# A cross-attention and feed-forward kernel: its query projection, the start of its score loop and its quantised weights rearranged

## What is computed

```python
q = (xq @ Wq.T + bq).reshape(B, N, HEADS, HEAD_DIM).transpose(0, 2, 1, 3)   # xq = layernorm(x)
k = (xk @ Wk.T + bk)...            # xk = xv = ctx_1024, 16 heads of 8
scores = jnp.einsum('bhnd,bhmd->bhnm', q, k) * scale
weights = jax.nn.softmax(scores, axis=-1)
...
def lpbq_dequant(w):               # blocks of 32 columns, 4 bits
    s = jnp.maximum(jnp.max(jnp.abs(wb), axis=-1, keepdims=True) / qmax, 1e-12)
    wq = jnp.clip(jnp.round(wb / s), -qmax - 1.0, qmax) * s
```

## Time and profile before

| | |
|---|---|
| device time, median of 3 runs | 823.46 us (821.6 to 823.87) |
| the profiled execution | 828.05 us, span 826.3 us |
| busy share of the span | PE 84%, DVE 71%, ACT 65%, POOL 50% |
| score loop, first and last start of its exponentials (L627) | 54.2 to 387.8 us |
| clock granted to TensorE, mean of the span | 0.923 |

### The profile page before, as it was taken

One profiled execution on the slowest core, in us unless ns is written; L12 is line 12 of the kernel. 1 busy time (PEld: TensorE's weight loads), 2 busy tenths in 40 slices (PEclk: granted clock), 3 DMA queues, 4 the chain that ended last, 5 costly groups with the idle time before them and its releaser, 6 DMA issues.

```text
span 826.3 us, 24071 instructions
## 1 busy us (share of the span) xinstructions
PE 697.6 (84%) x8999; PEld 498.9 (60%) x8999; DVE 589.1 (71%) x1092; ACT 537.1 (65%) x1164; POOL 415.1 (50%) x492
## 2 busy tenths in 40 slices
PE   5777999999999999997805688888788885899997
PEld 2255777777777777775402478777677783344443
DVE  4975788887888888887786667677777655566663
ACT  3354677777777777765452698789988872455554
POOL 1859577777777777700000135444445430466664
PEclk8898999999999999999856979899988896899999
DMA  6315544444444444230400405432540440212100
GB/s 198 106 38 164 143 126 133 131 130 132 129 132 129 131 130 132 66 71 8 183 0 25 207 2 176 173 119 79 205 184 3 155 155 2 75 39 77 38 1 23
DMA packets 26545, 85.75 MB, mean 104 GB/s; under 512 B 5780, under 2 KB 7316, under 8 KB 26468
## 3 DMA queue, kind: packets, MB, share of 16 engines
q1 hardware_dynamic: 26472, 84.77, 32.5%
HBM read 65.46 MB, written 0.46 MB: 80 GB/s over the span
## 4 chain that ended last, share of the span: by engine, by line
PE 51%; DVE 15%; POOL 12%; ACT 9%; issue 7%; SPq 3%; DMA 2%; POOLq 0%; DVEq 0%; ACTq 0%
POOL ctx_lo L601 8%; PE ps L1341 8%; PE ps L1358 7%; PE ps L1372 7%; PE ps L1605 5%; ACT c_prob L766 4%; PE ps L1328 4%; PE ps L1589 3%; PE ps L1317 2%; PE ps L1377 2%; ACT w0T L766 2%; SPq L439 2%; DVE tile_max L853 1%; PE ps L1623 1%; DVE amax_part L1077 1%
## 5 line engine op out<-in xcount | busy, mean ns | idle before, releaser
L853 DVE TENSOR_REDUCE tile_max<-ps 128x1 f32<-128x500 f32 x336 | 214.7, 674 | 52.0 <-PE ps L1341 51.2
L627 ACT ACTIVATE probs<-ps 125x896 f32<-125x896 f32 x192 | 175.3, 916 | 95.5 <-PE ps L1358 94.5
L1341 PE MATMUL ps<-k_hi,qdiag 128*128 128x500 f16 x336 | 130.4, 390 | 7.7 <-DVE tile_max L853 6.5
L766 ACT ACTIVATE c_prob<-ps,c_bias,row_scale 125x56 f32<-125x56 f32 x384 | 116.1, 479 | 3.0 <-DVE c_bias L1164 2.7
L578 POOL TENSOR_TENSOR c_prob<-c_prob,c_weight 125x672 f32<-125x672 f32 x32 | 41.9, 1312 | 133.7 <-DVE c_weight L1178 133.7
L1358 PE MATMUL ps<-qstack,kstack 98*125 98x224 f16 x768 | 107.1, 263 | 0.4
L601 POOL TENSOR_TENSOR ctx_lo<-ctx_hi,ctx_lo 128x448 f16<-128x448 f32 x64 | 71.9, 1124 | 70.5 <-ACT ctx_lo L811 70.5
L1358 PEld LDWEIGHTS ps<-qstack,kstack 98*125 98x125 f16 x768 | 86.6, 137 | 21.3 <-ACT probs L627 2.8
L1372 PE MATMUL ps<-probs,v_aug 125*32 125x168 f32 x1536 | 75.4, 314 | 3.3 <-ACT probs L627 2.5
L1659 PE MATMUL ps<-ctx_lo 128*128 128x448 f16 x192 | 68.5, 357 | 6.6 <-DVE ctx_hi L1276 2.8
L534 POOL TENSOR_TENSOR rows_in<-rows_in 125x768 f32<-125x768 f32 (+2 forms) x96 | 68.8, 717 | 7.5
(11 more groups left out here) (264 smaller groups left out, 1706.3 us busy)
## 6 DMA issues: line engine op xcount, KB each, us to landing
row_tiles<-in_ctx_rows_wide SPq DMA_DIRECT2D x40, 774.0 KB, 5.7
ctx<-in_ctxT SPq DMA_DIRECT2D x16, 750.0 KB, 5.4
rows_in<-in_ctx_rows SPq DMA_DIRECT2D x16, 750.0 KB
kstack<-k_hi SPq DMA_DIRECT2D x128, 93.8 KB, 3.2
kstack<-k_lo SPq DMA_DIRECT2D x64, 93.8 KB, 3.1
ctx_hi<-in_wg SPq DMA_DIRECT2D x8, 256.0 KB, 2.7
ctx_hi<-in_wu SPq DMA_DIRECT2D x8, 256.0 KB, 3.0
ctx_hi<-in_wd SPq DMA_DIRECT2D x8, 256.0 KB, 3.4
```

What stands on the lines that cost most here:

```text
L627: nc.scalar.activation(probs[c % RING_P][0:CH, :].rearrange("p (k w) -> p k w", k=2), score_tile(c)[0:CH], ACT.Exp, scale=float(HD) ** -0. ...
L766: last = nc.scalar.activation(c_prob[n % PROBS][:, c, :], ps[0:CH, 2 * (n % 2) + c // 6, bass.ts(c % 6, TOK)], ACT.Exp, bias=c_bias[n % 2] ...
L853: nc.vector.reduce_max(tile_max[:, u % MAXT, u // MAXT:u // MAXT + 1], ps[:, MAXB + (u + p) % 2, 0:KCOLS], AX.X).then_inc(max_done, 1)
L1341: nc.tensor.matmul(ps[:, MAXB + (u + p) % 2, 0:KCOLS], qdiag[p][:, bass.ts(t, 128)], k_hi[p][:, bass.ts(j, KCOLS)], start=True, stop=True) ...
```

## The change

- The queries are projected once. `q_lo`, the low part, is written by VectorE beside q_hi. The repeated rows of `q_rep` are filled by DMAs: eight issued by ACT (from q_hi) and four by SP (from q_lo). `wq_rep` and `bq_rep` and their loads are gone.
- On ACT `context_high(1)` and on POOL `split(1, 1)` come behind the queries. The third part of batch 0's keys comes right behind the queries on TensorE, ACT and VectorE.
- On SP the stacks of batches 0 and 1 come ahead of loads 2 and 3, and the row loads are spread anew.
- The quantised weights are loaded straight into `w0T`, scaled and rounded in place beside batch 14 (VectorE at c = 2 and c = 7, POOL at the end of its turns), turned beside batch 15 (TensorE, c = 0) into three PSUM banks and copied back by ACT in three pieces after its first exponential.

```diff
         normed = early[:, 0:T]
-        w0 = early[:, T:T + 3 * FFN0].rearrange("p (m i) -> p m i", m=3)
-        w0_blocks = early[:, T:T + 3 * FFN0].rearrange("p (k i) -> p k i", i=WBLOCK)
-        wq_rep = early[:, 2048:2048 + 3 * 128].rearrange("p (g r) -> p g r", g=GROUPS)
+        q_lo = early[:, T:T + T // 2].bitcast(F16)
+        w0 = w0T[:].rearrange("p (m k) i -> p m (k i)", m=3)
+        w0_blocks = w0T[:].rearrange("p k (b i) -> p (k b) i", i=WBLOCK)
         wqT, wkT, wvT = (early[:, 2432 + 128 * i:2432 + 128 * (i + 1)] for i in range(3))
...
                 stack(b, p)
-                if isinstance(b, int) and b == 0:
-                    load_rows(1)
                 load_rows(b + 2)
-            turn(0, 0)
-            turn(1, 1)
+            sp.wait_ge(q_lo_done, 2)
+            for g in range(GROUPS):
+                sp.dma_start(q_rep[2 * GR:3 * GR, g, :], q_lo[GR * g:GR * (g + 1), :]).then_inc(q_rep_loaded, 16)
+            stack(0, 0)
+            load(2, 0)
+            load_rows(1)
+            stack(1, 1)
+            load(3, 1)
+            load_rows(2)
+            load_rows(3)
             sp.dma_start(pick_sum[:], dram["pick_sum"]).then_inc(picks_loaded, 16)
...
             split(0, 0)
-            split(1, 1)
             pool.wait_ge(params, PARAMS)
...
-            pool.wait_ge(w0_step, 3)
-            nc.gpsimd.tensor_tensor(w0_blocks, w0_blocks, blocks(w0_inv), ALU.mult).then_inc(w0_divided, 1)
-            pool.wait_ge(q_hi_done, 2 + 2 * GROUPS)
-            pool.wait_ge(q_lo_done, 2 * GROUPS)
+            pool.wait_ge(q_rep_loaded, 16 * 3 * GROUPS)
             stacked_queries(0, 0)
-            pool.wait_ge(w0_step, 4)
-            nc.gpsimd.tensor_tensor(w0_blocks, w0_blocks, blocks(w0_scale), ALU.mult).then_inc(w0_rounded, 1)
+            split(1, 1)
             plain_queries(1, 1)
...
             stacked_queries(15, 1)
+            pool.wait_ge(w0_step, 3)
+            nc.gpsimd.tensor_tensor(w0_blocks, w0_blocks, blocks(w0_inv), ALU.mult).then_inc(w0_divided, 1)
+            pool.wait_ge(w0_step, 4)
+            nc.gpsimd.tensor_tensor(w0_blocks, w0_blocks, blocks(w0_scale), ALU.mult).then_inc(w0_rounded, 1)
...
-            for b in range(2):
+            def context_high(b):
...
-                if b == 0:
-                    act.wait_ge(ready, 3)
-                    layernorm_sd(0)
-                    act.wait_ge(constants, 1)
-                    k_high(0, 0, 0)
-                    k_high(0, 0, 1)
...
-            act.wait_ge(params, PARAMS)
...
+            context_high(0)
+            act.wait_ge(ready, 3)
+            layernorm_sd(0)
+            act.wait_ge(constants, 1)
+            k_high(0, 0, 0)
+            k_high(0, 0, 1)
...
-            for i in range(2 * GROUPS):
-                act.wait_ge(q_ready, i + 3)
-                g, h = i // 2, i % 2
-                nc.scalar.activation(q_rep[:, g, bass.ts(h, HALF)], ps[0:3 * GR, (2 + i) % 4, 0:HALF], ACT.Identity,
-                                     bias=bq_rep[:, g:g + 1]).then_inc(q_hi_done, 1)
...
+            act.wait_ge(q_hi_done, 2)
+            for r in range(2):
+                for g in range(GROUPS):
+                    nc.scalar.dma_start(q_rep[GR * r:GR * (r + 1), g, :], q_hi[GR * g:GR * (g + 1), :]).then_inc(q_rep_loaded, 16)
+            context_high(1)
...
-                if c == 8:
-                    act.wait_ge(w0_turned, 3)
-                    nc.scalar.copy(w0T[:].rearrange("p (k m) i -> p k (m i)", k=3), ps[:, 0:3, 0:3 * 128]).then_inc(w0_done, 1)
...
+            def turned_weights():
...
+                act.wait_ge(w0_turned, 1)
+                nc.scalar.copy(w0T[:, 0:4, :], ps[:, TURNED[0], :].rearrange("p (k i) -> p k i", k=4))
+                nc.scalar.copy(w0T[:, 4:8, :], ps[:, TURNED[1], :].rearrange("p (k i) -> p k i", k=4))
+                nc.scalar.copy(w0T[:, 8, :], ps[:, TURNED[2], 256:384]).then_inc(w0_done, 1)
...
+                    if batches == 0 and c == 0:
+                        turned_weights()
...
+            for i in range(2):
+                dve.wait_ge(q_hi_done, i + 1)
+                nc.vector.scalar_tensor_tensor(out=q_lo[:, bass.ts(i, HALF)], in0=ps[:, i, 0:HALF], scalar=bias_qkv[:, 0:1],
+                                               in1=q_hi[:, bass.ts(i, HALF)], op0=ALU.add, op1=ALU.subtract).then_inc(q_lo_done, 1)
+            k_low(0, 0, 2)
             dve.wait_ge(params, PARAMS)
             nc.vector.tensor_copy(ident[:], ident32[:]).then_inc(ready, 1)
-            step(nc.vector.tensor_reduce(w0_scale[:], w0_blocks, AX.X, ALU.max, apply_absolute_value=True), w0_step, 1)
-            step(nc.vector.tensor_scalar(w0_scale[:], w0_scale[:], 1.0 / 7.0, 1e-12, ALU.mult, ALU.max), w0_step, 2)
-            nc.vector.reciprocal(w0_inv[:], w0_scale[:]).then_inc(w0_step, 1)
-            for i in range(2 * GROUPS):
-                g, h = i // 2, i % 2
-                dve.wait_ge(q_hi_done, i + 3)
-                rows = slice(2 * GR, 3 * GR)
-                dst = q_rep[rows, g, bass.ts(h, HALF)]
-                nc.vector.scalar_tensor_tensor(out=dst, in0=ps[rows, (2 + i) % 4, 0:HALF], scalar=bq_rep[rows, g:g + 1],
-                                               in1=dst, op0=ALU.add, op1=ALU.subtract).then_inc(q_lo_done, 1)
-            k_low(0, 0, 2)
-            dve.wait_ge(w0_divided, 1)
-            nc.vector.tensor_scalar(w0, w0, MAGIC, MAGIC, ALU.add, ALU.subtract).then_inc(w0_step, 1)
             for c in range(NCH):
...
-            def main(b, p, batches=2):
+            def quantised_weights(c):
+                if c == 2:
+                    step(nc.vector.tensor_reduce(w0_scale[:], w0_blocks, AX.X, ALU.max, apply_absolute_value=True), w0_step, 1)
+                    step(nc.vector.tensor_scalar(w0_scale[:], w0_scale[:], 1.0 / 7.0, 1e-12, ALU.mult, ALU.max), w0_step, 2)
+                    nc.vector.reciprocal(w0_inv[:], w0_scale[:]).then_inc(w0_step, 1)
+                if c == 7:
+                    dve.wait_ge(w0_divided, 1)
+                    nc.vector.tensor_scalar(w0, w0, MAGIC, MAGIC, ALU.add, ALU.subtract).then_inc(w0_step, 1)
+            def main(b, p, batches=2, also=None):
                 for c in range(NCH):
+                    if also:
+                        also(c)
                     later = 1 if c < AHEAD else 2
...
                 nc.tensor.matmul(ps[:, i, 0:HALF], wqT, normed[:, bass.ts(i, HALF)], start=True, stop=True).then_inc(q_ready, 1)
-            for i in range(2 * GROUPS):
-                g, h = i // 2, i % 2
-                wait(pe, q_lo_done, i - 3)
-                if i == 2:
-                    pe.wait_ge(q_hi_done, 2)
-                nc.tensor.matmul(ps[0:3 * GR, (2 + i) % 4, 0:HALF], wq_rep[:, g, :], normed[:, bass.ts(h, HALF)],
-                                 start=True, stop=True).then_inc(q_ready, 1)
-                if i == 1:
-                    keys(0, 2)
+            keys(0, 2)
             pe.wait_ge(ready, 7)
...
                     shift(0, 0)
-                if c == 8:
-                    pe.wait_ge(q_lo_done, 2 * GROUPS)
-                    pe.wait_ge(w0_rounded, 1)
-                    for i in range(9):
-                        last = nc.tensor.transpose(ps[:, i // 3, bass.ts(i % 3, 128)], w0[:, i // 3, bass.ts(i % 3, 128)], ident32[:])
-                        if i % 3 == 2:
-                            last.then_inc(w0_turned, 1)
-            pe.wait_ge(w0_done, 1)
...
+            def turn_weights():
+                pe.wait_ge(w0_rounded, 1)
+                pe.wait_ge(v_done, NV * BATCH)
+                pe.wait_ge(max_done, UNITS * BATCH)
+                for i in range(3 * F0):
+                    last = nc.tensor.transpose(ps[:, TURNED[i // 4], 256 * (i // 8) + 128 * (i % 4):][:, 0:128], w0T[:, i, :], ident32[:])
+                last.then_inc(w0_turned, 1)
             def beside_last(c):
+                if c == 0:
+                    turn_weights()
                 if c == 3:
+                    pe.wait_ge(w0_done, 1)
                     pe.wait_ge(picks_loaded, 16)
```

More of the change, by code:

```diff
@@ L131, in build @@
         wv_lo = sbuf("wv_lo", [128, 128], F16, stack=sa)
-        bq_rep = sbuf("bq_rep", [3 * GR, GROUPS], stack=sa)
         bias_qkv = sbuf("bias_qkv", [128, 3], stack=sa)
@@ L256, in build @@
             sem("ln_" + n) for n in ("mean", "centred", "squared", "var", "sd", "rstd", "spread", "out"))
-        q_ready, q_hi_done, q_lo_done = sem("q_ready"), sem("q_hi_done"), sem("q_lo_done")
+        q_ready, q_hi_done, q_lo_done, q_rep_loaded = sem("q_ready"), sem("q_hi_done"), sem("q_lo_done"), sem("q_rep_loaded")
         q_built, qdiag_built = sem("q_built"), sem("qdiag_built")
@@ L360, in build @@
         PROJ = (MAXB + 1, MISC)
+        TURNED = (*PROJ, MAXB)
         def LATE(i):
@@ L414, in build @@
         k_list = [(wkT, "wkT"), (wvT, "wvT"), (bias_qkv[:], "bias_qkv")]
```

(6 more changed lines are left out.)

## The result

The changed kernel takes 830.53 us (median of 5 runs, 829.41 to 831.94) against 823.46 (5 runs, 821.6 to 826.66): a ratio of 1.0088, 95% interval 1.0066 to 1.0109. It is 7.07 us slower. In two later pairings the same two programs gave 1.0129 and 1.0066 (experiments e0, e9). The profiled execution took 831.94 with a span of 830.1, where that of before took 828.05 and 826.3.

A forecast was written before the change was run, and what follows sets the result against it. The prediction took TensorE to bound the score loop, with POOL's prologue and SP's queue order setting batch 2's start. Prologue +3.9 and tail +2.4 gave +6.3 on the 823.46 median: 829.8 us, range 825 to 834.

The forecast's parts named there:

- q_rep: Prologue: q_hi ready about 22.6, then ScalarE's eight DMA issues at 0.63 each; q_rep complete at 30.5 (bounds 27.3, 35).
- rival of cheap issues: Prologue: ScalarE's eight DMAs leave almost at once, q_rep lands at 27.3, POOL's chain moves 3.2, total 826.6; chance 0.15.
- Split of batch 2: Prologue, POOL: batch 2's context is split at 68.1, today 68.0, so nothing gained; TensorE must wait for it.
- Landing of rows 2: Prologue, SP's queue: rows 2, behind context 3's load, take 9.4 and land at 77.9 (bounds 76.6 and 78).
- Split of batch 3, kstack, gap: Prologue: batch 3's split at 92.3, batch 2's kstack complete at 102.6, a new TensorE gap of some 7 us.
- Prologue: Up to batch 2's c = 2 tile, at 111.05 instead of 107.14: loses 3.9 us (bounds -0.6 to +8.5).
- Batch 14: VectorE's reduce and two small operations at c = 2 all reach TensorE: +2.0 us (bounds 1.4 and 2.2).
- Batch 15: Transposes and copies between exp 0 and exp 1 cost +1.7; TensorE's wait before the output projection gives back 1.27.
- The sum: Whole kernel: prologue 3.9 plus tail 2.4 gives +6.3, forecast 829.8 us on the median's scale.
- the wait for the gather: Batch 15: TensorE's 1.27 wait before the output projection for ctx, counted as -1.27 since these delays leave the gather untouched.

The follow-up runs named there:

- e0: The changed kernel again, nothing edited, beside the kernel before: 835.47 us, ratio 1.0129.
- e9: The changed kernel once more, nothing edited, beside the kernel before in another pairing: 828.84 us, ratio 1.0066.
- e1: Changed kernel with load_rows(2) ahead of load(3, 1) in SP's queue: 822.35 us, ratio 0.9973 to the kernel before.
- e3: Changed kernel with its weight work cut into pieces across batches 14 and 15, all still computed: 829.14 us, ratio 1.0058 to the kernel before.
- e2: Changed kernel without the preparation of the quantised weights beside batches 14 and 15: 829.12 us, ratio 1.0068 to the kernel before.
- e4: Changed kernel with POOL's row squares and SP's row loads one batch later: 811.42 us, ratio 0.9848 to the kernel before.
- e8: Changed kernel with load_rows(2) ahead of load(3, 1) and without the quantised weights' preparation: 821.67 us, ratio 0.9973 to the kernel before.
- e11: Changed kernel with row squares one batch later, weight work cut up, output projection at c = 9 of batch 15, not c = 8: 805.61 us, ratio 0.9781.
- e7: Changed kernel with ScalarE's rounding of context 1 before its DMA issues and POOL's split(1, 1) before batch 0's stacked queries: 827.08 us, ratio 1.0037.

## Why the prediction was right

The forecast was 829.8 (825 to 834), the measured time 830.53. As a difference it was +6.3; the three pairings gave +7.1, +11.4 (e0, whose 835.47 lies above the range) and +5.4 (e9). The mechanism is the one that was forecast, shown by e1 to e3; that the number came within 0.7 is in part luck. Step by step:

- **q_rep.** Forecast 30.5, landed 28.9. ScalarE's issues cost 0.61 to 0.62 each (one 0.77), as taken from SP's 0.59; all began 1.4 sooner than reckoned, since q_hi is complete at 21.9, not 22.6, and the first issue runs beside k_high instead of behind it. The rival of cheap issues (27.3) is excluded: the eight took 5.27. The Trainium skill's sentence (DMA: Bandwidth & Descriptors, Issuing engines are not separate DMA queues) that the issue is usually small does not hold for this copy of 0.61 and 2.18.
- **Split of batch 2.** Forecast 68.1, ended at 66.3: 1.6 for q_rep, and little else. TensorE indeed stood waiting for it, the first gap.
- **Landing of rows 2.** 9.4 taken from the earlier trace rows, bounds 8.04 and 9.4; 10.16 in the chain (10.09 in e0, 10.25 in e9). The bound was too narrow by 0.8; the mechanism is shown by e1.
- **Split of batch 3, kstack, gap.** 92.3 forecast and 91.4 measured, 102.6 and 101.27, a gap of 7 and 5.7. TensorE's wait of 3.19 for the split of batch 3 is not in the forecast; it is hidden by the one behind it. From landing to the c = 2 tile 8.45 and 8.59.
- **Prologue.** +3.9 forecast; +2.7 in the trace of after, +1.6 and +4.8 in e0 and e9, mean +3.0. Here the errors partly cancel: q_rep 1.6 too late, the transfer 0.8 too short.
- **Batch 14.** +2.0 forecast, +2.2 measured. Its bounds (1.4 to 2.2) were too narrow: they priced the stall and not the clock behind it, with which it is +3.7 in e0, and +5.3 in e4 with POOL in the way.
- **Batch 15.** +1.7 and the wait of 1.27 regained, as forecast, and then 0.8 more between the projection and the reduce, which the forecast lacks. It is not the weights, since e2 has the same 0.8. It goes with the clock, which falls 12.9 us behind the start of the projection in before (at 395.9) and 10.2 in after (at 398.3); the last matmuls ahead of the reduce then take longer (before, then after). e4, where it falls at 12.9 too, has none of the 0.8.

```profile
395.34 1.15 PE L1499 MATMUL ps<-rstd,spread 128*128 128x210 f32 x4
```

```profile
400.65 1.73 PE L1505 MATMUL ps<-rstd,spread 128*128 128x210 f32 x4
```

- **The sum.** +6.3 forecast, +7.07 measured in the medians, +5.9 at the reduce of the trace. The trace of the whole span says only +3.9, since the low-clock stretches of the slot loop move it by several us; no single span could have told the forecast from half of it.

What the forecast did not see is in e2 and e8: the wait for the gather, which it counted as a gain of 1.27 for the change, is a limit on what any saving in batches 14 and 15 can bring.

## What to carry over

Where two loads share a queue and one of them waits for a late buffer, ask which of them the engine that sets the pace needs first: here one exchange of two lines was worth 11 to 12 us at batch 2, more than the 9.9 that the saved work brings. A head start is only worth what the next engine in the chain lets through, so take the slowest engine's work (here the row squares) out of the chain first; then the single projection is worth its 10 us, and e11 ends 2.2% below the kernel before. When a stage is costed, add to a stall of TensorE the clock that may fall behind it (1.3 to 1.6 us here), and look for the wait that will stand in its place.

## What the runs showed of the hardware

- The same program differs by up to 0.8% in its median from one pairing to another (828.84 to 835.47), while the kernel before stays at 823.3 to 824.1. A wait of 1.66 in batch 14 was followed by a clock of 1.00 in one execution and 0.57 in another; at the projection, waits of 1.27 and 1.40 were followed by full clock (1.58), waits of 1.60, 2.21, 2.68 and 2.85 by half (2.85 to 2.98). The waits alone do not decide it.
- ScalarE's sequencer issues DMAs beside an instruction that runs already, and only what stands behind them waits: in after the cast of context 1 starts at 27.41, 4.63 idle; in e7, where it stands ahead of them, it runs at 22.74 while the issues go on.
- A small VectorE `tensor_scalar` of SBUF on SBUF went from 0.18 to 1.77 and ended with the POOL operation that had begun 0.07 before it; in the kernel before it took 2.27 and ended with POOL's. A reduce beside POOL kept its 1.34. The Trainium skill (SBUF — State Buffer, Who interferes with whom) says that the two share ports under an exclusive lock, held for a whole instruction; the rows agree.
- A transfer of rows took 7.8 to 9.0 without a context load just ahead of it (e1, e7; 8.04 before) and 10.0 to 10.3 behind one in the same queue (after, e0, e2, e3, e7, e9).
- The last of twelve copies into kstack landed after 2.18 in after and after 4.60 in e9, the same program (3.82 in e3, 4.29 in e7). Why is not shown.
